# A perceiver layer on one Trainium2 core: order of the work at batch boundaries of the cross attention and at group boundaries of the self attention

## The chip, the cores and the metric

The kernel runs on one core of a Trainium2 chip. The metric is the device time of one execution, in microseconds (us). The kernel before takes 922.68 us (median of 3 runs, 922.39 to 923.87). A core has a matmul engine (PE), a vector engine (DVE), an activation engine (ACT), a general engine (POOL) and a sync engine (SP) that issues DMAs. Each works through its own list of instructions in order; they meet only at semaphores. A semaphore wait holds back everything that stands behind it on its engine.

## The reference

Three stages, each added to x (8 batches of 64 rows by 512):

```python
# cross attention: context of 1601 keys per batch, 16 heads, a latent of 32
C_q = Q @ Wq_d;  C_kv = K @ Wkv_d
scores = einsum('bnhl,bkl->bhnk', (C_q @ W_qk).reshape(b, n, H, LKV), C_kv) / sqrt(LKV)
out = einsum('bhnk,bkhd->bnhd', softmax(scores), (C_kv @ Wv_u).reshape(b, nkv, H, HD))
# self attention: 32 query heads in 8 groups of 4, 512 selected cache keys and 64 new ones
out = softmax(q @ k_full.T / sqrt(HD)) @ v_full;  out @ wo.T
# feed forward, with weights that need a mean over the whole matrix
coeff = mean(abs(w - base));  W = base + coeff * sign(w - base)
out = (silu(h @ W1.T) * (h @ W3.T)) @ W2.T
```

## The kernel before

Everything is written by hand: each engine has one function body per stage, and the order in it is the order on the engine. Most fp32 operands are split in a high and a low part, and products are made of three passes.

**Cross attention.** The loop runs over 8 batches `b`. For a batch there are 13 tiles of keys (`KT`). `scores(b, t)` on PE makes a tile's scores in two halves of 512 columns, `exponential` on ACT turns each half into probabilities, `add_tile` on POOL sums probability tiles in groups (`GROUPED`) for the denominators, and `values(b, units)` on PE multiplies the probabilities with the latent keys. The maximum that is subtracted is not taken from these scores. It is computed one batch ahead: between the tiles of batch `b`, PE makes 16 pairs of products for batch `b + 1` (`max_scores`, called as `maximum(i)`), in two buffers, and DVE reduces each (`take_max`, L1003). When all 16 are reduced, DVE combines them (`negate_max`, L1009), PE turns the result to a row with 8 transposes (`turn_max`, L706), and ACT copies that row of 1024 values, the *shift row*, into the query operand (`shift_row`, L919), where it takes part in `scores` as one more row of the contraction. So `scores(b + 1, 0)` cannot start before the shift row of `b + 1` stands.

At the end of a batch PE also has `compress(b + 3)` (the latent keys of a later batch, only while `b + 3 < 8`), `natural(b + 3)`, and `tail_and_denominators(b)` (L758 and L745), which adds the last tile's values and multiplies all probability sums with ones. The latter waits for POOL's last sum. ACT then copies the denominators (`copy_den`, L926), in the next batch, behind its second tile.

**Self attention.** `head(g, i, ...)` is one step of a pipeline over 32 heads (group `g`, head `i` in it). In a step PE turns the probabilities of the last head (`turn_probs`, L1413 and L1422), makes scores for this one (`score`, L1401), projects queries of the next (`queries`, L1382), and multiplies with the values (`mix`, L1431 to L1440). In the step with `i = 0` of groups 1 to 7, PE also makes the output products of the group before, 48 matmuls (`output`, L1455). I call this the group boundary; there are 7. DVE then adds the four output tiles to x (`add_output`, L1808), and splits the new group's values (`values_low`, L1726 and L1728). POOL casts the values (L1886), waits for `values_low`, and then subtracts three pieces of the feed-forward weights and their bases (`w_piece`, L1908). ACT sums the absolute values of these three pieces (`abs_sum`, L1624) and makes the high part of the first output weight of the group (`output_weight_high`, L1645), which has to wait until the output products no longer read the old one. Behind both stands `turned_high` (L1637) of the next head, on which `turned_low` (DVE, L1742) and PE's third turn depend, since there are two buffers for turned probabilities.

## Time and profile before

| what | value |
|---|---|
| median of 3 runs | 922.68 us |
| profiled execution, its own time | 919.89 us |
| its span | 917.8 us |
| cross attention, batch loop | from about 44 to 286 us |
| keys and norm | 288 to 318 us |
| self attention | 318 to about 796 us |
| feed forward | to the end |
| PE busy | 93% |
| mean granted PE clock, share of 2.4 GHz | 0.985 |

The profile gives, for each instruction group, start, duration, and for an engine that sat idle how long and for whom it waited. A busy PE is not PE at its peak: the ends of matmuls are modelled, and short waits vanish in them. So the distance between starts says more than the busy time.

### The profile page before, as it was taken

The numbers are of one execution on the slowest core, as the hardware profiler recorded it, in microseconds if no ns is written. First come the engines' busy times: TensorE is split into PE (matmuls) and PEld (weight loads), VectorE is DVE, ScalarE is ACT, GpSimd is POOL, SyncE is SP. The second block draws the span as 40 slices with busy tenths as digits, with TensorE's granted clock in tenths as the row PEclk, the third lists the DMA queues.
The fourth block names the chain that finished last, engine by engine and source line by source line (L and its number), as shares of the span: only waits on it lengthen the run. The fifth ranks groups of instructions, "written<-read, shape, count | busy, mean of one in ns | idle before, by whom it ended". The sixth has DMA issues, their size and how long they took to land.

```text
span 917.8 us, 15508 instructions
## 1 busy us (share of the span) xinstructions
PE 851.7 (93%) x5338; PEld 650.9 (71%) x5338; DVE 603.3 (66%) x993; ACT 519.1 (57%) x1005; POOL 459.6 (50%) x294
## 2 busy tenths in 40 slices
PE   6898899888987889999999999999999999899998
PEld 4455455544433668888788887887878878788886
DVE  5965567555625268578486684776848759768884
ACT  5655546555554466386474774655746657555552
POOL 2698788786751054544444444345454454154430
PEclk9899999999999999999999999999999999999999
DMA  8654244104103515032050230501505002535531
GB/s 359 217 199 153 99 153 171 28 19 136 58 1 121 193 43 207 24 134 97 0 206 23 95 133 0 206 23 41 187 0 203 15 0 92 184 127 194 192 107 46
DMA packets 42338, 102.96 MB, mean 112 GB/s; under 512 B 7858, under 2 KB 12978, under 8 KB 41394
## 3 DMA queue, kind: packets, MB, share of 16 engines
q1 hardware_dynamic: 42002, 102.06, 31.7%
q8 instruction: 30, 0.49, 0.2%
q10 hardware_dynamic: 288, 0.26, 0.1%
q14 instruction: 18, 0.15, 0.1%
HBM read 96.95 MB, written 1.05 MB: 107 GB/s over the span
## 4 chain that ended last, share of the span: by engine, by line
PE 51%; POOL 5%; DVE 3%; issue 3%; ACT 2%; DMA 0%; SPq 0%; DVEq 0%; POOLq 0%; ACTq 0%
PE psum L1401 9%; PE psum L1382 9%; PE psum L1517 8%; PE psum L1413 5%; PE psum L1531 4%; POOL w_piece L1908 3%; PE psum L1440 3%; PE psum L1431 3%; PE psum L1455 3%; PE psum L1436 3%; ACT w_piece L1624 2%; PE psum L1422 1%; PE psum L1432 1%; PE psum L1434 1%; DVE probs_t_low L1742 1%
## 5 line engine op out<-in xcount | busy, mean ns | idle before, releaser
L1896 POOL TENSOR_TENSOR head_probs<-head_probs,inverse_den 128x576 f32<-128x576 f32 x128 | 147.5, 1153 | 203.7 <-DVE inverse_den L1749 203.7
L1003 DVE TENSOR_REDUCE max_part<-psum 128x1 f32<-128x804 f32 x128 | 121.2, 991 | 38.4 <-PE psum L698 38.0
L901 ACT ACTIVATE probs<-psum 128x512 f32<-128x512 f32 (+1 forms) x208 | 106.7, 608 | 47.4 <-PE psum L719 46.4
L1631 ACT ACTIVATE head_probs<-psum,neg_max 128x576 f32<-128x576 f32 x128 | 94.7, 740 | 46.2 <-DVE neg_max L1766 45.8
L1766 DVE TENSOR_REDUCE neg_max<-psum 128x1 f32<-128x576 f32 x128 | 96.9, 757 | 23.8 <-PE psum L1401 21.3
L567 POOL TENSOR_TENSOR prob_sums<-prob_sums,probs 128x1024 f32<-128x1024 f32 (+1 forms) x42 | 100.2, 2386 | 18.4 <-ACT probs L901 14.1
L1742 DVE TENSOR_TENSOR probs_t_low<-psum,probs_t_high 128x512 fp32r<-128x512 f32 x124 | 84.8, 684 | 16.6 <-ACT probs_t_high L1637 15.6
L1413 PE MATMUL psum<-ident,head_probs 128*128 128x128 f32 x496 | 78.7, 274 | 16.5 <-DVE probs_t_low L1742 15.1
L719 PE MATMUL psum<-q_t,c_t 97*128 97x512 f32 (+1 forms) x208 | 76.1, 445 | 14.2 <-ACT q_t L919 7.1
L1401 PE MATMUL psum<-k_high,query_t_high 128*128 (+1 forms) x256 | 86.5, 338 | 1.9 <-DVE query_t_low L1721 1.4
L567 POOL TENSOR_TENSOR prob_sums<-probs 128x1024 f32<-128x1024 f32 x30 | 71.3, 2380 | 23.9 <-ACT probs L901 23.8
L1413 PEld LDWEIGHTS psum<-ident,head_probs 128*128 128x128 f32 x496 | 60.6, 141 | 28.5 <-issue 20.2
L1916 POOL TENSOR_TENSOR ffn_quant<-ffn_raw 128x1536 f32<-128x1536 f32 x13 | 45.6, 3510 | 67.4 <-DVE ffn_w_low L1830 26.9
L1401 PE MATMUL psum<-k_high,query_t_low 128*128 (+1 forms) x256 | 75.7, 296 | 0.0
L698 PE MATMUL psum<-c_t,q_t 96*128 96x402 f32 x256 | 73.5, 374 | 2.3 <-DVE max_part L1003 1.7
L1401 PE MATMUL psum<-k_low,query_t_high 128*128 (+1 forms) x256 | 75.6, 295 | 0.0
L1637 ACT ACTIVATE probs_t_high<-psum 128x512 fp32r<-128x512 f32 x124 | 72.9, 588 | 0.5 <-PE psum L1422 0.5
L698 PEld LDWEIGHTS psum<-c_t,q_t 96*128 96x128 f32 x256 | 43.9, 191 | 37.8 <-DVE max_part L1003 23.3
L719 PEld LDWEIGHTS psum<-q_t,c_t 97*128 97x128 f32 (+1 forms) x208 | 38.5, 191 | 38.0 <-ACT probs L901 27.8
L1908 POOL TENSOR_TENSOR w_piece<-w_piece 128x1024 f32<-128x1024 f32 x21 | 49.7, 2397 | 23.6 <-DVE value_low L1728 23.6
L1645 ACT ACTIVATE wo_t_high<-wo_nat 128x512 fp32r<-128x512 f32 x32 | 20.0, 626 | 72.4 <-PE psum L1455 72.4
L1808 DVE TENSOR_TENSOR x<-psum,x 128x512 f32<-128x512 f32 x32 | 22.1, 690 | 46.9 <-PE psum L1455 46.9
(227 smaller groups left out, 1948.2 us busy)
## 6 DMA issues: line engine op xcount, KB each, us to landing
ctx_t_odd<-in_ctx_dram SPq DMA_DIRECT2D x4, 3202.0 KB, 11.0
ffn_raw<-in_L_ffn_w_dram SPq DMA_DIRECT2D x42, 256.0 KB, 3.9
ffn_raw<-in_L_ffn_mean_w_dram SPq DMA_DIRECT2D x42, 256.0 KB, 4.1
w_piece<-in_L_ffn_w_dram SPq DMA_DIRECT2D x21, 512.0 KB, 6.5
w_piece<-in_L_ffn_mean_w_dram SPq DMA_DIRECT2D x21, 512.0 KB, 7.5
cache<-in_ctx_dram SPq DMA_DIRECT2D x3, 3202.0 KB, 10.8
wq_nat<-in_L_attn_wq_dram SPq DMA_DIRECT2D x32, 256.0 KB, 7.4
wo_nat<-in_L_attn_wo_dram SPq DMA_DIRECT2D x32, 256.0 KB, 3.2
```

Source lines behind the costliest of these rows:

```text
L567: pool.tensor_tensor(total[rows, :], (prob_buffer(b, t - 1) if first else total)[rows, :], prob_buffer(b, t)[rows, :], ALU.add).then_inc(s ...
L698: mm = pe.matmul(psum[:, bank + k, 0:PIECE_KEYS], q_t[0:SHIFT, b, 2 * qt:2 * qt + 2, :].rearrange("p h n -> p (h n)"), c_t[0:SHIFT, b % 3, ...
L719: pe.matmul(psum[0:rows_of(t), n % SCORE_BANKS, :], lhs, rhs[:, half * BANK:(half + 1) * BANK], start=True, stop=True).then_inc(s_sb, 1)
L901: act.activation(prob_buffer(b, t)[0:rows, half * BANK:(half + 1) * BANK], psum[0:rows, n % SCORE_BANKS, :], ACT.Exp, scale=XSCALE).then_i ...
L1003: dve.tensor_reduce(max_part[:, qt, pair:pair + 1], psum[:, bank:bank + 2, 0:PIECE_KEYS], AX.XY, ALU.max).then_inc(s_max, 1)
L1382: mm = pe.matmul(psum[:, head_bank(i), :], wq_t[a][:, c, :], (xh, xl)[b][:, c, :], start=(k == 0), stop=(k == 3 * DC - 1))
L1401: mm = pe.matmul(psum[:, bank, 0:HALF], q_t[a][:, qt * P:(qt + 1) * P], (k_high, k_low)[b][:, keys], start=(step == 0), stop=(step == 2))
L1413: mm = pe.transpose(bank[:, t * P:(t + 1) * P], probs[:, qt, t * P:(t + 1) * P], core.ident[:, :])
L1631: act.activation(probs[:, qt, :].rearrange("p (a k) -> p a k", a=2), psum[:, 2 * (qt % 2):2 * (qt % 2) + 2, 0:HALF], ACT.Exp, bias=neg_max ...
L1742: dve.tensor_tensor(probs_t[1][:, 0:ST, qt * P:(qt + 1) * P], psum[:, turn_bank(qt), :].rearrange("p (t q) -> p t q", t=ST), probs_t[0][:, ...
L1766: dve.tensor_reduce(neg_max[:, qt:qt + 1], psum[:, 2 * (qt % 2):2 * (qt % 2) + 2, 0:HALF], AX.XY, ALU.max, negate=True).then_inc(s["max"], 1)
L1896: pool.tensor_tensor(probs[:, qt, :], probs[:, qt, :], rden[:, qt:qt + 1].to_broadcast([P, KEYS]), ALU.mult).then_inc(s["norm"], 1)
```

## The change

Four edits, all of order.

1. Group boundary, ACT: the three absolute sums stand ahead of the output weight's high part. Group boundary, DVE: `values_low` stands ahead of all four `add_output`.
2. Cross attention, shift row: PE signals after the first four transposes and after the last four. ACT copies the row as two halves of 512. `scores(b, 0)` waits, half by half, for the half that it reads.
3. Cross attention, maxima: from `maximum(5)` on, each is issued one place earlier; one pair instead of two stands behind the last `values` of a batch.
4. Batches 5, 6 and 7: `tail_and_denominators(b)` stands ahead of `turn_max(b + 1)`, and ACT copies these denominators at the end of the batch, ahead of the shift row. Batches 0 to 4 keep `tail_and_denominators` behind the first scores of the next batch.

```diff
@@ tensor engine, turn_max
-                mm.then_inc(s_mt, 1)
+                    if qt % 4 == 3:
+                        mm.then_inc(s_mt, 1)
@@ tensor engine, scores
-                    if t == 0 and half == 0:
-                        pe.wait_ge(s_shift, b + 1)
+                    if t == 0:
+                        pe.wait_ge(s_shift, 2 * b + half + 1)
@@ tensor engine, batch loop
                 maximum(4)
+                maximum(5)
                 values(b, range(0, 2))
                 for t in range(6, 10):
-                    maximum(t - 1)
+                    maximum(t)
                     scores(b, t)
-                maximum(9)
+                maximum(10)
                 values(b, range(2, 4))
                 for t in range(10, KT):
-                    maximum(t)
+                    maximum(t + 1)
                     scores(b, t)
-                maximum(KT)
+                maximum(KT + 1)
                 values(b, range(4, 6))
-                maximum(KT + 1)
                 maximum(KT + 2)
                 if b + 3 < BATCH:
                     compress(b + 3)
-                if lead:
                     turn_max(b + 1)
-                if b + 3 < BATCH:
                     natural(b + 3)
+                else:
+                    tail_and_denominators(b)
+                    if lead:
+                        turn_max(b + 1)
                 if lead:
                     scores(b + 1, 0)
                     scores(b + 1, 1)
-                tail_and_denominators(b)
+                if b + 3 < BATCH:
+                    tail_and_denominators(b)
@@ activation engine, shift_row
-                act.wait_ge(s_mt, b + 1)
-                act.activation(q_t[SHIFT:STACK, b, :, :].rearrange("p (a h) n -> p a (h n)", a=2),
-                               psum[SHIFT:STACK, TURN_BANK:TURN_BANK + 2, :], ACT.Copy).then_inc(s_shift, 1)
+                for half in range(2):
+                    heads = slice(half * XH // 2, (half + 1) * XH // 2)
+                    act.wait_ge(s_mt, 2 * b + half + 1)
+                    act.activation(q_t[SHIFT:STACK, b, heads, :].rearrange("p h n -> p (h n)"),
+                                   psum[SHIFT:STACK, TURN_BANK + half, :], ACT.Copy).then_inc(s_shift, 1)
@@ activation engine, batch loop
-                    if t == 1 and b > 0:
+                    if t == 1 and 0 < b < BATCH - 2:
                         copy_den(b - 1)
...
                 if b + 3 < BATCH:
                     compressed(b + 3)
+                else:
+                    copy_den(b)
                 if b + 1 < BATCH:
                     shift_row(b + 1)
...
-            copy_den(BATCH - 1)
@@ activation engine, head
-                if this and i == 0:
-                    output_weight_high(g, i)
                 if last and i == 0:
                     for k in range(3):
                         abs_sum(g, k)
+                if this and i == 0:
+                    output_weight_high(g, i)
@@ vector engine, head
-                if i == 0 and last:
-                    add_output(g, 0, turn_bank(0))
                 if this and i == 0:
                     values_low(g)
                 if i == 0 and last:
-                    for qt in range(1, TT):
+                    for qt in range(TT):
                         add_output(g, qt, turn_bank(qt))
```

The other waits on `s_mt` and `s_shift` have their counts doubled. Line numbers below the edits move by a few.

On ACT, at the last group boundary (`w_piece...` are the absolute sums, `wo_t_high` the output weight, `mixed_t_high` the result of `mix`, `probs_t_high` the turned probabilities), before:

```order
L1583 ACTIVATE wq_t_high<-wq_nat 128x512
L1612 ACTIVATE mixed_t_high<-psum 128x512
L1645 ACTIVATE wo_t_high<-wo_nat 128x512
L1624 ACTIVATE w_piece_4090,abs_part<-w_piece_4090 128x1024
L1624 ACTIVATE w_piece_4091,abs_part<-w_piece_4091 128x1024
L1624 ACTIVATE w_piece,abs_part<-w_piece 128x1024
L1637 ACTIVATE probs_t_high<-psum 128x4x128
```

and now:

```order
L1590 ACTIVATE wq_t_high<-wq_nat 128x512
L1619 ACTIVATE mixed_t_high<-psum 128x512
L1631 ACTIVATE w_piece_4114,abs_part<-w_piece_4114 128x1024
L1631 ACTIVATE w_piece_4115,abs_part<-w_piece_4115 128x1024
L1631 ACTIVATE w_piece,abs_part<-w_piece 128x1024
L1652 ACTIVATE wo_t_high<-wo_nat 128x512
L1644 ACTIVATE probs_t_high<-psum 128x4x128
```

The output weight has moved behind the three sums; nothing else moved.

On DVE, at the same boundary (`x<-psum,x` is `add_output`), before:

```order
L1734 TENSOR_TENSOR mixed_t_low<-psum,mixed_t_high 128x512
L1808 TENSOR_TENSOR x<-psum,x 128x512
L1726 TENSOR_TENSOR value_low<-cache,value_high 128x512
L1728 TENSOR_TENSOR value_low<-v_new,value_high 64x128
L1808 TENSOR_TENSOR x<-psum,x 128x512 x3
L1766 TENSOR_REDUCE neg_max<-psum 128x1
```

and now:

```order
L1741 TENSOR_TENSOR mixed_t_low<-psum,mixed_t_high 128x512
L1733 TENSOR_TENSOR value_low<-cache,value_high 128x512
L1735 TENSOR_TENSOR value_low<-v_new,value_high 64x128
L1813 TENSOR_TENSOR x<-psum,x 128x512 x4
L1773 TENSOR_REDUCE neg_max<-psum 128x1
```

The low values no longer stand behind the first output tile.

On PE, at the end of batch 5 (L733 is the last `values`, `c_t,q_t` with 402 columns are the maxima, `max_row` the turn, `c_nat` and `ones_by_latent` behind it the tail and the denominators), before:

```order
L733 MATMUL psum<-probs,c_nat 32x512 x8
L698 MATMUL psum<-c_t,q_t 128x402 x4
L706 MATMUL psum<-ident,max_row 97x128 x8
L719 MATMUL psum<-q_t,c_t 128x512 x4
L758 MATMUL psum<-probs,c_nat 32x512
L745 MATMUL psum<-prob_sums,ones_by_latent 32x512
L758 MATMUL psum<-probs,c_nat 32x512
L745 MATMUL psum<-prob_sums,ones_by_latent 32x512 x9
L698 MATMUL psum<-c_t,q_t 128x402 x2
```

and now:

```order
L734 MATMUL psum<-probs,c_nat 32x512 x8
L698 MATMUL psum<-c_t,q_t 128x402 x2
L759 MATMUL psum<-probs,c_nat 32x512
L746 MATMUL psum<-prob_sums,ones_by_latent 32x512
L759 MATMUL psum<-probs,c_nat 32x512
L746 MATMUL psum<-prob_sums,ones_by_latent 32x512 x9
L706 MATMUL psum<-ident,max_row 97x128 x8
L720 MATMUL psum<-q_t,c_t 128x512 x4
L698 MATMUL psum<-c_t,q_t 128x402 x2
```

Twelve matmuls went from behind the next batch's first scores to ahead of the turn, and one pair of maxima went ahead of the values.

## Rows read from the trace of the kernel before

**Rows 1.** First part of the page: busy us, share, instructions.

```profile
PE 851.7 (93%) x5338; PEld 650.9 (71%) x5338; DVE 603.3 (66%) x993; ACT 519.1 (57%) x1005; POOL 459.6 (50%) x294
```

**Rows 2.** Chain that ended last, in order of time: start, duration, what.

```profile
420.97 2.05 PE psum L1382 x9
...
432.30 2.06 PE psum L1382 x9
...
456.73 2.05 PE psum L1382 x9
```

**Rows 3.** Timeline, one group boundary: start, duration, engine, what, [idle before <-releaser].

```profile
438.22 0.69 DVE L1734 TENSOR_TENSOR mixed_t_low<-psum,mixed_t_high 128x512 fp32r<-128x512 f32 x1 [1.69 <-ACT mixed_t_high L1612]
...
440.31 0.69 DVE L1808 TENSOR_TENSOR x<-psum,x 128x512 f32<-128x512 f32 x1 [1.40 <-PE psum L1455]
...
441.52 0.28 DVE L1728 TENSOR_TENSOR value_low<-v_new,value_high 64x128 fp32r<-64x128 f32 x1
441.96 7.11 POOL L1908 TENSOR_TENSOR w_piece<-w_piece 128x1024 f32<-128x1024 f32 x3 [3.37 <-DVE value_low L1728]
...
448.28 0.60 PE L1413 MATMUL psum<-ident,head_probs 128*128 128x128 f32 x4
...
448.54 0.63 ACT L1645 ACTIVATE wo_t_high<-wo_nat 128x512 fp32r<-128x512 f32 x1 [10.35 <-PE psum L1455]
...
452.20 0.58 ACT L1637 ACTIVATE probs_t_high<-psum 128x512 fp32r<-128x512 f32 x1
...
453.64 0.63 PE L1413 MATMUL psum<-ident,head_probs 128*128 128x128 f32 x4 [2.06 <-DVE probs_t_low L1742]
```

**Rows 4.** Waits of the whole span: us in total, times, longest.

```profile
PE psum L1413 <- DVE probs_t_low L1742: 15.1, 9, 2.1
```

**Rows 5.** Windows: length, busy us (instructions) PE PEld DVE ACT POOL, granted clock, DMA.

```profile
437.39:448.28 10.89, 10.89 (x50) 8.96 (x48) 3.56 (x6) 0.60 (x1) 7.17 (x5) 1.00 0.00 0
549.10:575.00 25.90, 23.84 (x119) 20.32 (x119) 12.22 (x22) 12.12 (x27) 13.15 (x10) 0.94 0.00 0
```

**Rows 6.** Timeline of a batch boundary that stands for batches 0 to 4.

```profile
130.10 1.00 PE L698 MATMUL psum<-c_t,q_t 96*128 96x402 f32 x4
130.77 1.90 DVE L1003 TENSOR_REDUCE max_part<-psum 128x1 f32<-128x804 f32 x2 [1.42 <-PE psum L698]
131.82 2.79 PE L650 MATMUL psum<-ctx_t_odd,wkv_d 128*32 128x384 f32 x32 [0.72 <-DVE max_part L1003]
...
134.99 1.12 PE L706 MATMUL psum<-ident,max_row 128*97 128x128 f32 x8
...
136.15 1.02 ACT L919 ACTIVATE q_t<-psum 1x1024 fp32r<-1x1024 f32 x1 [0.47 <-PE psum L706]
...
137.31 0.94 PE L719 MATMUL psum<-q_t,c_t 97*128 97x512 f32 x3 [0.70 <-ACT q_t L919]
```

**Rows 7.** Timeline of the boundary from batch 5 to batch 6.

```profile
222.16 2.34 POOL L567 TENSOR_TENSOR prob_sums<-prob_sums,probs 65x1024 f32<-65x1024 f32 x1
...
224.56 1.12 PE L706 MATMUL psum<-ident,max_row 128*97 128x128 f32 x8 [1.83 <-DVE max_row L1009]
...
226.88 2.16 PE L719 MATMUL psum<-q_t,c_t 97*128 97x512 f32 x4 [1.20 <-ACT q_t L919]
...
227.59 2.08 ACT L901 ACTIVATE probs<-psum 128x512 f32<-128x512 f32 x4 [0.86 <-PE psum L719]
...
229.84 2.58 PE L745 MATMUL psum<-prob_sums,ones_by_latent 128*32 128x512 f32 x17
...
232.50 1.21 ACT L926 ACTIVATE u_all<-psum 64x512 f32<-64x512 f32 x2 [2.83 <-PE psum L745]
...
234.38 0.50 PE L719 MATMUL psum<-q_t,c_t 97*128 97x512 f32 x1 [0.71 <-ACT probs L901]
```

**Rows 8.** Window in that boundary, columns as in Rows 5.

```profile
226.98:230.40 3.42, 3.42 (x12) 1.30 (x16) 0.00 (x0) 2.08 (x4) 0.65 (x1) 0.50 0.56 182
```

**Rows 9.** Timeline of the boundary from batch 6 to batch 7.

```profile
264.92 0.50 PE L719 MATMUL psum<-q_t,c_t 97*128 97x512 f32 x1 [1.06 <-ACT probs L901]
```

More of the change, by code:

```diff
@@ L679, in max_scores @@
                     pe.wait_ge(s_qlo[b > 1], 2 * (b // 2 if b > 1 else 1))
-                    wait(pe, s_shift, b)
+                    wait(pe, s_shift, 2 * b)
                 elif i == 1 and b == 0:
@@ L772, in mix @@
                 elif b + 1 < BATCH:
-                    pe.wait_ge(s_shift, BATCH)
+                    pe.wait_ge(s_shift, 2 * BATCH)
                 else:
@@ L1007, in negate_max @@
                 dve.wait_ge(s_max, MAXIMA * (b + 1))
-                wait(dve, s_mt, b)
+                wait(dve, s_mt, 2 * b)
                 dve.tensor_reduce(max_row[:, :, SHIFT], max_part[:, :, :], AX.X, ALU.max,
```

## The prediction

> **What bounds the kernel now.** I read the busy shares first: PE is busy 93% of the span, the next engine 66% [rows 1]. So a change pays where PE waits, or where another engine paces PE. The chain in order of time then shows where PE's rhythm breaks. In the self attention the last nine query matmuls of a head start every 11.33 us (420.97 to 432.30); across a group boundary the distance is 24.43 us (432.30 to 456.73) [rows 2]. The 48 output matmuls explain 10.89 us of it [rows 5]. 24.43 - 11.33 - 10.89 leaves 2.21 us, of which 2.06 us shows as PE's wait ahead of the third turn, at 453.64 [rows 3]. The list of waits has this pair with 15.1 us in 9 waits, longest 2.1 [rows 4]: 7 boundaries at about 2.06 us make 14.4 of them.
>
> The timeline tells why. ACT is idle 10.35 us until the outputs are done, makes the output weight at 448.54, then the three sums, and reaches the turned probabilities at 452.20 only [rows 3]. PE made them at 448.28. ACT does work here that could have been done while it sat idle.
>
> In the cross attention the timeline of a batch boundary shows PE waiting 0.72 us for a DVE maximum before `compress` and 0.70 us for the shift row [rows 6]. At the end of batch 5 there is no `compress` to cover the maxima: PE waits 1.83 and 1.20 us there and 0.71 us for an exponential held up by the denominators' copy [rows 7].
>
> **Group boundary.** `mixed_low` runs at 438.22 and takes some 0.6 us. `values_low` now follows it: start about 438.83. Before, 441.52 + 0.28 is its end and POOL starts 0.16 later; from the first half's start (0.6 before 441.52, so 440.92) to POOL is 1.04 us. So POOL starts at about 439.87 in place of 441.96, and its three differences (7.11 us) end at 446.98 [rows 3]. From 448.54 to 452.20 ACT makes the weight copy and three sums, 3.66 us: 0.54 and three times 1.04. So each sum now waits for its difference and the last ends at 446.98 + 0.1 + 1.04 = 448.1, ahead of 448.54, where ACT starts the weight copy anyway. The copy ends at 449.08 and turned probabilities start there in place of 452.20: 3.12 us earlier [rows 3]. PE's wait was 2.06, so it goes, with 1.0 us to spare. What is late next is PE itself. The first output tile is added to x at 440.31 as before, since `values_low` ends at 439.7, so PE's third output tile is not held up. Behind the sums on ACT now stands the weight copy, and behind it the turned probabilities; a late third difference would be covered by 0.4 us of ACT's wait and then by that 1.0. I take 2.2 us for each of 7 boundaries, 15.4 us. Bounds: 7 x 2.06 = 14.4 when only the shown wait goes, and above 1.4 us more, since between 549.10 and 575.00 one boundary took 25.90 us with a granted clock of 0.94 [rows 5] in place of 24.43: a dip of the clock to 1.2 GHz just behind this wait. Lower bound: 1.0 us for each, 7 us, if something unseen stands behind.
>
> **Maxima moved up.** DVE needs 0.95 us for a maximum (1.90 for two) and sets the pace between the `values`; each `values` leaves it idle 1.42 us whatever stands ahead, as PE is in order [rows 6]. So DVE's last maximum does not end earlier. What changes is the end on PE: the last `values` now begins and ends about 0.95 us later (131.05 in place of 130.10), but one pair stands behind it, 0.4 us, not two and a wait. `compress` starts at 131.45 in place of 131.82: 0.37 us, bounded by 0 and by the wait of 0.72. This counts for batches 0 to 4. The scores of tiles 10 to 12 come 0.9 us later by it; POOL's sums have slack there in those batches.
>
> **Shift row by halves.** Before, the row is copied from 136.15 to 137.17 and the scores start at 137.31, with PE's turn begun at 134.99 [rows 6]. The first four transposes are done about 0.45 earlier than the last, so the first half can start at about 135.7 (ACT's copy of the compressed keys ends there too). A half of 512 costs 0.54 to 0.60: the two copies of 64x512 take 1.21 [rows 7]. Both are done at 136.8 to 136.9, and the first score goes at 136.5, when `natural` lets PE go. From there ACT's exponentials pace the start, which come 1.02 + 136.15 - 136.8 = 0.4 earlier. I take 0.42; bounds 0 and the wait of 0.70. Batches 0 to 4: 5 x (0.37 + 0.42) = 4.0 us, and 0.3 for the very first row; bounds 0 and 7.1.
>
> The Trainium skill (ScalarE: Activation LUTs, What ACT_TABLE_LOAD costs) has an ACTIVATE with immediate scale at 186 ns + 0.833 ns per element. It agrees with the row of 1.02 us for 1024, and it speaks against the split: two halves would be 1.22 us, 0.2 more than one. By it the term would be 0.25 and not 0.42 at each of 7 rows, 1.2 us in all.
>
> **Late denominators, batches 5 and 6.** First the price. PE now waits for POOL's last sum ahead of the turn. That sum ends at 222.16 + 2.34 = 224.50, and comes 0.9 later because its scores do: 225.4 [rows 7]. The last group of denominator matmuls follows. The matmuls take 0.15 us a record with a part of them at half clock (17 in 2.58), 8 records to a group, so 1.2; I take 0.9 at full clock [rows 7]. The turn starts at 226.4 in place of 224.56. ACT copies denominators from 226.55 to 227.78 (1.21) and only then the half rows, so the first score starts at 228.5, not 226.88: 1.6 us worse. Then the return. Behind the first four scores there are no denominators, and ACT goes from exponential to exponential at 0.52 (four in 2.08) without a copy between. The last score of tile 3 waits for the fifth exponential: 229.0 + 5 x 0.52 + 0.2 = 231.8, against 234.38 [rows 7]. Gain 2.6 us. At the next boundary that last score stands 30.54 later, at 264.92, so the same chain gives 262.3; there is no maximum between the scores, which saves 0.5 more: 261.8 [rows 9], gain 3.1. Together 5.7 us. Bounds: the shown waits on ACT's copy and PE alone, 1.2 each, 2.4; and 1.0 more than I take if the clock stays up. Between 226.98 and 230.40 it was at 0.50 [rows 8], the level of 1.2 GHz, after the two waits of 1.83 and 1.20 us.
>
> What follows the batch loop starts its loads behind a barrier, so gains there pass on whole.
>
> **The sum.** 15.4 + 4.0 + 0.3 + 5.7 = 25.4 us. On the profiled execution's own time, 919.89, that is 894.5. The median of the runs is 922.68, 0.3% above it, and I take the gain off that: 897.3. Some runs may hold more clock dips at boundaries, like the one above, which would go too; I say 897.
>
> **Rivals.** (a) *Only the group boundary pays.* Cross attention gives back what it gains: DVE's pace is unchanged and the late denominators hold the turn. For it: the first score of batch 6 is 1.6 us later by my own sum. Against it: 3 us of PE work and a 1.2 us copy leave the stretch behind it. 922.7 - 15.4 = 907.
>
> (b) *The group boundary pays half.* The turned probabilities are early, but PE then waits for DVE, which has a row maximum ahead of the low part. For it: DVE makes a row maximum ahead of the low part, so an early ACT need not mean an early PE. Against it: the 24 ordinary heads have the same order and next to none of these waits [rows 4]. 7 x 1.1 + 10 = 17.7: 905.
>
> (c) *Slower: POOL's differences and DVE's additions get in each other's way.* POOL now runs beside three additions all through, and ACT's weight copy, the turned probabilities and PE stand behind the third sum. If each difference took twice as long, the third ended at 454.1, turned probabilities started at 455.8, 3.6 us later than before; 7 x 3.6 - 10 = 15 us slower, 938. It turns to slower when the third difference ends some 5 us later than I have it. Against it: the 7.11 us were measured beside three such additions already [rows 3].
>
> **How the numbers follow.** Forecast as worked out (892 to 903): 0.75. (a) and (b), 903 to 908: 0.18. Less than that gained, still faster by over 0.2%: 0.03. No change within 0.2% (about what a measurement of this kernel can tell from none; its three runs spread by 0.16%): 0.02. (c) and other slower ends: 0.02. Faster 0.96. The range of 891 to 906 leaves out some 0.2.
>
> **What would show it.** In the profile after, the distance of the query matmuls across a group boundary should be 22.2, with no wait of PE for `probs_t_low`; POOL's differences should start 2.1 us earlier against the outputs. A batch period should be 29.75 in place of 30.55. At the late boundaries PE should wait for a sum of POOL, then for the half rows. I am wrong if the boundary distance stays above 23, or if batches 5 to 7 take as long as before.

## The result and the profile after

The changed kernel takes 899.44 us (median of 4 runs, 895.99 to 901.27), the kernel before 923.27 us beside it (median of 4, 922.39 to 924.5): a ratio of 0.9737, 95% interval 0.9704 to 0.9769. The forecast was 897.0 in 891 to 906. The profiled execution is the slowest of the four, 901.27 us with a span of 899.2, while that of before, at 919.89, was faster than all the timed ones of before. So the two profiles differ by 18.6 us and the medians by 23.8.

The page of the profile after, its first part (busy us, share, instructions) and its chain by engine; before is [rows 1]:

```profile
PE 855.6 (95%) x5338; PEld 652.4 (73%) x5338; DVE 606.5 (67%) x993; ACT 522.6 (58%) x1013; POOL 459.1 (51%) x294
...
PE 60%; DVE 2%; POOL 1%; DMA 1%; ACT 1%; issue 0%; SPq 0%; POOLq 0%; DVEq 0%
```

The same work stands in a shorter span: 8 more ACTIVATEs (the halves), and PE 2 points busier.

**Group boundary.** The chain in order of time (start, duration, what), to be laid beside [rows 2]:

```profile
416.90 2.06 PE psum L1389 x9
...
428.24 2.05 PE psum L1389 x9
...
450.44 2.06 PE psum L1389 x9
```

11.34 us in a head as before, 22.20 across the boundary where it was 24.43. All seven measure 22.19 to 22.20. The timeline of that boundary (start, duration, engine, what, [idle before <-releaser]) answers to [rows 3]:

```profile
434.16 0.69 DVE L1741 TENSOR_TENSOR mixed_t_low<-psum,mixed_t_high 128x512 fp32r<-128x512 f32 x1 [1.68 <-ACT mixed_t_high L1619]
...
435.36 0.28 DVE L1735 TENSOR_TENSOR value_low<-v_new,value_high 64x128 fp32r<-64x128 f32 x1
435.80 7.11 POOL L1913 TENSOR_TENSOR w_piece<-w_piece 128x1024 f32<-128x1024 f32 x3 [1.28 <-DVE value_low L1735]
436.24 0.69 DVE L1813 TENSOR_TENSOR x<-psum,x 128x512 f32<-128x512 f32 x1 [0.61 <-PE psum L1462]
...
442.95 1.06 ACT L1631 ACTIVATE w_piece<-w_piece 128x1024 f32<-128x1024 f32 x1 [1.21 <-POOL w_piece L1913]
...
444.21 0.60 PE L1420 MATMUL psum<-ident,head_probs 128*128 128x128 f32 x4
444.47 0.63 ACT L1652 ACTIVATE wo_t_high<-wo_nat 128x512 fp32r<-128x512 f32 x1 [0.37 <-PE psum L1462]
445.01 0.58 ACT L1644 ACTIVATE probs_t_high<-psum 128x512 fp32r<-128x512 f32 x1
```

POOL starts 1.64 us behind `mixed_low`'s start, where it was 3.74, and takes 7.11 us as before. The last sum is over 0.37 us before the weight copy, whose wait is for PE. The turned probabilities follow PE's first turn by 0.80 us (445.01 less 444.21) in place of 3.92 [rows 3]. In the list of waits (us in total, times, longest) [rows 4] became two short waits, and what was ACT's idle time has a new name:

```profile
ACT w_piece L1631 <- POOL w_piece L1913: 45.6, 21, 4.1
...
PE psum L1420 <- DVE probs_t_low L1749: 0.8, 2, 0.6
```

**Batch boundary, batches 0 to 4.** The same engines as in [rows 6]:

```profile
130.96 1.92 PE L734 MATMUL psum<-probs,c_nat 128*32 128x512 f32 x16
132.82 0.63 PE L698 MATMUL psum<-c_t,q_t 96*128 96x402 f32 x2
133.38 2.79 PE L650 MATMUL psum<-ctx_t_odd,wkv_d 128*32 128x384 f32 x32
...
136.55 1.12 PE L706 MATMUL psum<-ident,max_row 128*97 128x128 f32 x8
...
137.27 1.07 ACT L925 ACTIVATE q_t<-psum 1x512 fp32r<-1x512 f32 x2
...
138.09 1.09 PE L720 MATMUL psum<-q_t,c_t 97*128 97x512 f32 x3
```

Neither wait of PE is left, neither the 0.72 ahead of `compress` nor the 0.70 for the row. The score starts 1.54 us behind the turn, not 2.32.

**Boundary from batch 5 to 6,** answering to [rows 7]:

```profile
222.90 2.36 POOL L567 TENSOR_TENSOR prob_sums<-prob_sums,probs 65x1024 f32<-65x1024 f32 x1
...
225.32 1.07 PE L746 MATMUL psum<-prob_sums,ones_by_latent 128*32 128x512 f32 x8 [0.35 <-POOL prob_sums L567]
226.31 1.12 PE L706 MATMUL psum<-ident,max_row 128*97 128x128 f32 x8
226.45 1.21 ACT L932 ACTIVATE u_all<-psum 64x512 f32<-64x512 f32 x2 [5.20 <-PE psum L746]
227.68 1.07 ACT L925 ACTIVATE q_t<-psum 1x512 fp32r<-1x512 f32 x2
228.41 1.66 PE L720 MATMUL psum<-q_t,c_t 97*128 97x512 f32 x4 [0.98 <-ACT q_t L925]
...
230.28 1.75 PE L720 MATMUL psum<-q_t,c_t 97*128 97x512 f32 x4
```

The turn is at 226.31 (forecast 226.4), ACT's copy at 226.45 (226.55), the first score at 228.41 (228.5). Batch 4's denominators are copied 0.16 us earlier than before (201.81 against 201.97), so the times of the two profiles can be laid side by side here. The last score of tile 3 ends at 232.03, before at 234.88 (234.38 and 0.50) [rows 7]; against the copy that starts the stretch in the table below that is 2.7 us earlier. The window of [rows 8] now holds a full clock. But one batch later the clock falls (windows: length, busy us (instructions) of PE, PEld, DVE, ACT, POOL, granted clock, DMA):

```profile
226.98:230.40 3.42, 2.43 (x12) 1.43 (x10) 0.00 (x0) 3.20 (x8) 0.00 (x0) 1.00 0.52 169
...
258.00:266.00 8.00, 8.00 (x52) 4.26 (x56) 1.05 (x3) 4.86 (x10) 6.79 (x3) 0.57 0.01 2
```

**Where the 18.6 us of the two profiles went.** Each stretch is the difference of two starts in the timeline or the chain: the first copy of compressed keys in the batch loop (52.18 before, 55.34 after), the copy of batch 4's denominators early in batch 5 (201.97, 201.81), the table load of the next stage (288.25, 285.08), the first and the 29th group of nine query matmuls. The later columns are the same stretches in kernels described below.

| stretch, us | before | after | one pair, single run (e7) | one pair, timed (e12) | late as before, timed (e13) | combined (e10) |
|---|---|---|---|---|---|---|
| start to first key copy | 52.18 | 55.34 | 54.97 | 54.14 | 53.53 | 54.88 |
| to batch 4's denominators, some five periods | 149.79 | 146.47 | 146.10 | 146.06 | 146.50 | 146.09 |
| to the next stage's table load | 86.28 | 83.27 | 79.59 | 83.97 | 83.43 | 81.13 |
| to the first query group | 51.72 | 52.99 | 50.61 | 51.71 | 50.39 | 53.00 |
| to the 29th, 7 group boundaries | 410.27 | 393.18 | 393.11 | 393.12 | 392.97 | 393.12 |
| to the end of the span | 167.56 | 167.95 | 168.22 | 168.80 | 167.78 | 167.88 |

After less before: +3.16, -3.32, -3.01, +1.27, -17.09, +0.39: -18.6. The second stretch is the same within 0.5 us in every kernel with the same order of work in it, and so is the fifth where the group boundary has its new order (392.9 to 393.2 us, e5 left out). With the old order the fifth holds one or two dips of the clock: 410.3 us before and in e6, 412.0 in e2. The other stretches differ by up to 4.4 us even between two runs of one program.

### The profile page after: what moved, and what is told of

Its sections match the earlier page's. It is cut to its first block, busy times and chain, and to the rows that moved or that the text cites. A ratio compares the mean times of both kernels' runs of the same rounds, so it can differ in the third digit from the quotient of the medians.

```text
span 899.2 us, 15523 instructions
## 1 busy us (share of the span) xinstructions
PE 855.6 (95%) x5338; PEld 652.4 (73%) x5338; DVE 606.5 (67%) x993; ACT 522.6 (58%) x1013; POOL 459.1 (51%) x294
## 4 chain that ended last, share of the span: by engine, by line
PE 60%; DVE 2%; POOL 1%; DMA 1%; ACT 1%; issue 0%; SPq 0%; POOLq 0%; DVEq 0%
PE psum L1408 11%; PE psum L1389 10%; PE psum L1524 9%; PE psum L1462 8%; PE psum L1420 6%; PE psum L1538 4%; PE psum L1447 3%; PE psum L1438 3%; PE psum L1443 3%; PE psum L1429 1%; PE psum L1441 1%; PE psum L1439 1%; DMA ffn_raw<-in_L_ffn_mean_w_dram 1%; POOL head_probs L1901 0%; POOL ffn_quant L1921 0%; POOL ffn_raw L1921 0%
## 5 line engine op out<-in xcount | busy, mean ns | idle before, releaser
L1010 DVE TENSOR_REDUCE max_part<-psum 128x1 f32<-128x804 f32 x128 | 121.1, 991 | 41.5 <-PE psum L698 41.1
L720 PE MATMUL psum<-q_t,c_t 97*128 97x512 f32 (+1 forms) x208 | 78.0, 449 | 8.4 <-ACT probs L905 5.7
L698 PE MATMUL psum<-c_t,q_t 96*128 96x402 f32 x256 | 75.3, 377 | 4.2 <-DVE max_part L1010 3.6
L1408 PEld LDWEIGHTS psum<-k_high,query_t_high 128*128 128x128 f32 x256 | 48.3, 189 | 2.7 <-DVE query_t_low L1728 1.8
```

Of the source, the lines that this page charges most:

```text
L698: mm = pe.matmul(psum[:, bank + k, 0:PIECE_KEYS], q_t[0:SHIFT, b, 2 * qt:2 * qt + 2, :].rearrange("p h n -> p (h n)"), c_t[0:SHIFT, b % 3, ...
L720: pe.matmul(psum[0:rows_of(t), n % SCORE_BANKS, :], lhs, rhs[:, half * BANK:(half + 1) * BANK], start=True, stop=True).then_inc(s_sb, 1)
L1010: dve.tensor_reduce(max_part[:, qt, pair:pair + 1], psum[:, bank:bank + 2, 0:PIECE_KEYS], AX.XY, ALU.max).then_inc(s_max, 1)
L1408: mm = pe.matmul(psum[:, bank, 0:HALF], q_t[a][:, qt * P:(qt + 1) * P], (k_high, k_low)[b][:, keys], start=(step == 0), stop=(step == 2))
```

## The experiments

Medians are of 4 runs and ratios are to the kernel before, timed beside them, unless the text says otherwise. A single run gives a time and a profile, but no interval.

**e1_group_only.** The kernel before with the two edits at the group boundary and nothing else.
```diff
-                if this and i == 0:
-                    output_weight_high(g, i)
                 if last and i == 0:
                     for k in range(3):
                         abs_sum(g, k)
+                if this and i == 0:
+                    output_weight_high(g, i)
```
(and the same hunk of `values_low` as in the change.)

> The kernel before with the two edits of the group boundary alone. Theory (the boundary pays 2.2 us, seven times): query matmuls 22.2 us apart across a boundary, no wait of PE for the low probabilities, and the whole faster by 15.4 us, ratio 0.983; up to 1.5 us more where the kernel before had a dip of the clock there. Rival (b) of the prediction (it pays half): distance 23.3, ratio 0.992.

Measured: 906.02 us against 924.11 (13 runs), 0.9802 (0.9774 to 0.983). All seven distances are 22.2, so rival (b), 23.3, falls. The stage of the seven boundaries takes 392.99 us. The median gain, 18.1 us, is above the theory's 15.4 and the 1.5 for a dip; the theory's ratio of 0.983 lies at the upper end of the interval.

**e2_cross_only.** The changed kernel with the group boundary as before (the hunk above undone on both engines).

> The changed kernel with the group boundary as in the kernel before, so only the three edits of the cross attention. Theory: batches 0 to 4 gain 0.67 us each (read from the profile after), the late boundaries up to 5.7 less what half clock in the last batch takes back, 2: in all 6 to 9 us, ratio 0.990 to 0.993. Rival (a) (the cross attention gives back what it gains): ratio 0.998 to 1.000. The distance of the query matmuls across a group boundary stays 24.4.

Measured: 917.82 us (10 runs), 0.9931 (0.9896 to 0.9965). Boundaries at 24.4, two at 25.9. The two gains, 18.1 and 6.3 us, make 24.4, the whole change 23.8: within the intervals they add up.

**e5_low_values_late, e6_sums_late.** The two halves of the group boundary's edit, each undone alone in the changed kernel, a single run each. e5 puts `values_low` behind the first output tile's addition again:
```diff
-                if this and i == 0:
-                    values_low(g)
                 if i == 0 and last:
-                    for qt in range(TT):
+                    add_output(g, 0, turn_bank(0))
+                if this and i == 0:
+                    values_low(g)
+                if i == 0 and last:
+                    for qt in range(1, TT):
```

> The changed kernel with the low values again behind the first output tile; the absolute sums stay ahead of the weight. Theory (POOL's third difference then ends at 449.1 on the clock of the kernel before, the sum at 450.2, the weight copy at 450.8, PE's third turn at 452.2): PE waits 0.6 us for the low probabilities, distance across a boundary 22.8. Rival (only the place of the sums counts, the low values are free to stand anywhere): 22.2. Rival (the low values carry it all): 24.4.

> The changed kernel with the output weight ahead of the absolute sums again; the low values stay ahead of the output tiles. Theory (ACT still starts its three sums only when the outputs are done, at 449.08): no gain at the boundary, distance 24.4 and PE's wait 2.06, though POOL's differences start 2.1 us earlier. Rival (POOL's earlier start pays by itself): a distance under 23.5.

Measured: e5 908.22 us, boundaries 22.84 to 22.98, the seven-boundary stage 398.17, 5.0 us longer than in the changed kernel. The distances are near the theory's 22.8, and both rivals fall. Its stretch behind batch 4 is 4.4 us longer too (87.70 against 83.27): the clock fell at both late boundaries, which this edit doesn't touch. e6, with the output weight ahead of the sums again, 917.10 us and 24.4 (one of 25.76). Their waits, e5's and then e6's:

```profile
PE psum L1420 <- DVE probs_t_low L1749: 4.5, 9, 0.6
```
```profile
PE psum L1420 <- DVE probs_t_low L1749: 15.2, 9, 2.1
```

With the weight first, the low values' move gains nothing: the wait is that of [rows 4] within 0.1 us. With the sums first, the wait falls to 0.6, and the low values' move takes that. So the sums' order is worth 1.5 us a boundary and the low values 0.7 on top, in this order only.

**e4_maxima_as_before, e8_row_whole.** In the changed kernel, the PE order of the maxima as before, and the shift row copied in one piece; a single run each.
```diff
-                for half in range(2):
-                    heads = slice(half * XH // 2, (half + 1) * XH // 2)
-                    act.wait_ge(s_mt, 2 * b + half + 1)
-                    act.activation(q_t[SHIFT:STACK, b, heads, :].rearrange("p h n -> p (h n)"),
-                                   psum[SHIFT:STACK, TURN_BANK + half, :], ACT.Copy).then_inc(s_shift, 1)
+                act.wait_ge(s_mt, 2 * b + 2)
+                act.activation(q_t[SHIFT:STACK, b, :, :].rearrange("p (a h) n -> p a (h n)", a=2),
+                               psum[SHIFT:STACK, TURN_BANK:TURN_BANK + 2, :], ACT.Copy).then_inc(s_shift, 2)
```

> The changed kernel with the maxima placed as in the kernel before. Theory: the steady batch period is 30.55 - 0.42 = 30.1 us (29.88 in the changed kernel), PE waits 0.72 us for a maximum ahead of the compress again, and at the late boundary POOL's last sum is 0.8 us earlier, so the first score of batch 6 comes 0.8 us earlier. Rival (the maxima carry the batch's gain, the halves nothing): period 30.5. Rival (the maxima cost more than they bring): period at or under 29.9.

> The changed kernel with the shift row copied whole, by one activation. Theory: the period is 0.3 to 0.4 us longer than the changed kernel's 29.88, and PE waits 0.7 us for the row at each boundary. Rival (the fixed price of a second activation eats the gain): the same period within 0.1.

Measured: 899.04 and 906.97 us. The batch period is 30.55 before, 29.88 after, 30.16 in e4 and 30.35 in e8. So, each with the other in place, the maxima are worth 0.28 and the halves 0.47 a batch; that makes 0.75, and the two together moved the period by 0.67. In e4 the first score of batch 6 comes 0.33 us earlier against the copy of batch 4's denominators (26.27 us behind it, 26.60 in the changed kernel), not the 0.8 that was expected. The old waits are back, in e4 and in e8 (timelines, PE):

```profile
133.03 2.79 PE L650 MATMUL psum<-ctx_t_odd,wkv_d 128*32 128x384 f32 x32 [0.73 <-DVE max_part L1010]
```
```profile
136.55 0.93 PE L720 MATMUL psum<-q_t,c_t 97*128 97x512 f32 x3 [0.76 <-ACT q_t L923]
```

e8's total is 7.5 us above the changed kernel's median and 5.7 above its profiled run, and its periods account for 2.3; the stretch behind batch 4 takes 90.0 us, against 83.3, with dips of the clock at both late boundaries.

**e7_one_pair_only, e12_one_pair_timed.** One program, run twice: only the pair of maxima ahead of the last `values` is moved up, the other five stay where they were.
```diff
                 maximum(4)
-                maximum(5)
                 values(b, range(0, 2))
                 for t in range(6, 10):
-                    maximum(t)
+                    maximum(t - 1)
                     scores(b, t)
-                maximum(10)
+                maximum(9)
                 values(b, range(2, 4))
                 for t in range(10, KT):
-                    maximum(t + 1)
+                    maximum(t)
                     scores(b, t)
+                maximum(KT)
                 maximum(KT + 1)
```

> The changed kernel in which only the last but one pair of maxima is moved ahead of the last values; all others stand as in the kernel before. Theory (what pays is that one pair and not two stands behind the last values): period 29.9 as in the changed kernel, and the late scores no longer come 0.9 us later. Rival (two pairs in a row ahead of the last values make PE wait a step of DVE, 0.95 us, that the gain does not cover): period over 30.2.

> The kernel in which only one pair of maxima is moved up (ahead of the last visits to the values) and the rest is as in the changed kernel; seen once at 894.7 us with a batch period of 29.80, now timed in rounds. Theory A (moving the other five pairs makes each visit to the values wait for VectorE's maximum, 0.08 us a batch, nothing else): 5 periods by 0.08 us, 0.4 us below the changed kernel's 899.4, that is 899; the 894.7 was a run with few dips of the clock. Theory B (the shorter wait of TensorE at the boundaries also keeps its clock up): 895 to 896 as the median, and the changed kernel is beaten by 3 to 4 us.

Measured: 894.71 us in the single run, 899.54 (896.56 to 903.05) timed, 0.9745 (0.9702 to 0.9788): the same as the changed kernel. The period is 29.80 in the single run's profile and in the timed one alike, 0.08 less than with six pairs moved, and the first score of batch 6 comes 0.6 us earlier against the copy of batch 4's denominators than in the changed kernel (0.9 was expected). So one pair does all that moving the maxima does. The 894.7 was luck: the two profiles of this one program differ by 5.2 us, 4.4 of them behind batch 4 (79.59 against 83.97 in the table). The last batch in the single run (e7), then in the timed profile (e12) (windows, columns as before):

```profile
256.00:264.00 8.00, 7.55 (x61) 3.42 (x61) 1.05 (x3) 5.99 (x13) 6.97 (x3) 1.00 0.01 2
264.00:272.00 8.00, 7.69 (x42) 2.63 (x46) 0.00 (x0) 5.88 (x12) 7.16 (x4) 1.00 0.00 0
```
```profile
256.00:264.00 8.00, 8.00 (x54) 3.64 (x54) 1.05 (x3) 3.94 (x8) 7.01 (x3) 0.57 0.01 2
264.00:272.00 8.00, 7.78 (x31) 2.57 (x27) 0.00 (x0) 4.25 (x9) 4.68 (x2) 0.79 0.00 0
```

Up to there the two agree: from turn to turn 27.19 us in both, the first score of batch 7 then 2.11 and 2.10 us behind its turn. Then one run stays at 1.00 and the other falls to 0.5. Whoever had compared single runs would have called this a gain of 5 us.

**e3_late_as_before, e13_late_timed.** Again one program twice: the changed kernel with the late denominators as before.
```diff
                 if b + 3 < BATCH:
                     compress(b + 3)
+                if lead:
                     turn_max(b + 1)
+                if b + 3 < BATCH:
                     natural(b + 3)
-                else:
-                    tail_and_denominators(b)
-                    if lead:
-                        turn_max(b + 1)
                 if lead:
                     scores(b + 1, 0)
                     scores(b + 1, 1)
-                if b + 3 < BATCH:
-                    tail_and_denominators(b)
+                tail_and_denominators(b)
```

> The changed kernel with the late denominators (batches 5 to 7) placed as in the kernel before. Theory: from the sixth batch's start to the end of the cross attention it takes some 5 us more than the changed kernel, 2.7 of it at the boundary from batch 5 to 6 where PE waits 1.8 us for the row of maxima and the exponentials are held up by the denominators' copy. Rival (a): the difference is under 1 us, since the turn no longer waits for POOL's sum. Clock: if the two waits of PE ahead of the first scores (1.8 and some 0.7 us) bring the clock down, it is at 1.2 GHz behind the boundary from 5 to 6 here and not in the changed kernel.

> The changed kernel with the late denominators as before (copied behind the second exponential of the next batch, products behind the first scores), seen once at 899.1 us, now timed in rounds. Theory A (as predicted, the reorder is worth 2.6 us at the boundary from batch 5 to 6 and 3.1 at the next): 899.4 and 5.7 us, 905. Theory B (the waits removed at the two boundaries are given back by the clock and by ScalarE's copy ahead of the half rows): 899 to 900, no difference to the changed kernel.

Measured: 899.10 us in the single run, 897.57 (896.65 to 898.6) timed, 0.9726 (0.9696 to 0.9757). Theory A, 905, falls, and so does the "some 5 us" that was expected of the single run: the stretch behind batch 4 takes 83.7 and 83.4 us in the two, 83.3 in the changed kernel. The boundary from 5 to 6 without the reorder but with halves and moved maxima (timeline of the timed profile, PE):

```profile
222.59 1.12 PE L706 MATMUL psum<-ident,max_row 128*97 128x128 f32 x8 [1.29 <-DVE max_row L1012]
224.04 1.66 PE L720 MATMUL psum<-q_t,c_t 97*128 97x512 f32 x4 [0.33 <-ACT q_t L922]
...
226.10 2.31 PE L746 MATMUL psum<-prob_sums,ones_by_latent 128*32 128x512 f32 x17
...
228.81 0.85 PE L720 MATMUL psum<-q_t,c_t 97*128 97x512 f32 x3
...
230.36 0.50 PE L720 MATMUL psum<-q_t,c_t 97*128 97x512 f32 x1 [0.70 <-ACT probs L902]
```

PE's waits of 1.83 and 1.20 us [rows 7] are 1.29 and 0.33 here, and the clock in the windows from 222 to 252 us is 1.00 in both runs. From the denominators' copy of batch 5 to that of batch 6 it takes 28.47 us, 30.54 in the kernel before (263.04 less 232.50), and 27.83 in the changed kernel (254.28 less 226.45). Before, then the changed kernel (timelines):

```profile
232.83 0.85 PE L719 MATMUL psum<-q_t,c_t 97*128 97x512 f32 x3
...
263.04 1.21 ACT L926 ACTIVATE u_all<-psum 64x512 f32<-64x512 f32 x2 [3.01 <-PE psum L745]
```
```profile
254.28 1.21 ACT L932 ACTIVATE u_all<-psum 64x512 f32<-64x512 f32 x2 [5.19 <-PE psum L746]
```

Of the 2.7 us that the changed kernel gains there, 2.07 come without the late denominators; these add 0.64. The last score of tile 3 says the same: against the copy of batch 4's denominators it ends 2.08 us earlier than before in e13, and 2.69 in the changed kernel. Where the 2.07 lie can be read too. The first score stands 1.45 us behind the turn, not 2.32: 0.87. From it to the three scores behind the denominators it is 4.77 us (228.81 less 224.04), not 5.95 (232.83 less 226.88) [rows 7]: 1.18, over the same matmuls, which before ran in part at the half clock of [rows 8]. So 0.87 is the row's wait, and 1.18 the dip.

**e10_combined.** One pair moved, and the denominators of batches 5 to 7 copied by VectorE behind the copy of u.
```diff
-                else:
-                    copy_den(b)
...
                 copy_u(b)
+                if b + 3 >= BATCH:
+                    copy_den(b)
```

> The changed kernel with two further edits: of the six pairs of maxima only one is moved up (the one ahead of the last visits to the values), and the denominators of batches 5 to 7 are copied by VectorE behind the copy of u, where ScalarE did it ahead of the shift row. Theory A (ScalarE's copy of 1.21 us stands ahead of the half rows at the three late boundaries, and VectorE's copy beside it costs nothing there): 2 boundaries by up to 1.2 us, so about 2 us below the kernel with one pair moved alone, which showed 894.7 in one look: 892 to 893, and the first score of batch 6 follows the turn by 0.98 us less the copy, some 1.2 us earlier against the batch's start than in the changed kernel. Theory B (VectorE's next maxima are late by its two copies, as they were by each piece of VectorE's work at this place): no gain or a loss of up to 1 us, 895 to 896. Theory C (the lost time at the late boundaries is clock alone): the same as the kernel with one pair, with the stretch from batch 5's denominators to the next stage's table load at 80 to 84 us as the dips have it.

Measured: 896.16 us (894.07 to 898.2), 0.97 (0.9668 to 0.9732). The half rows follow the turn at once, with the first score's wait down to 0.33:

```profile
224.81 1.12 PE L706 MATMUL psum<-ident,max_row 128*97 128x128 f32 x8
226.26 1.66 PE L720 MATMUL psum<-q_t,c_t 97*128 97x512 f32 x4 [0.33 <-ACT q_t L925]
```

The score comes 1.45 us behind the turn, not 2.10. From the turn of batch 6 to that of batch 7 it is 26.53 us, 27.19 in both runs with one pair alone, at a full clock in all three: 0.66, of the 1.2 expected; theory A's total, 892 to 893, isn't reached. Its median is 3.3 us below the changed kernel's, but the intervals overlap, so that it beats it is likely and not shown. VectorE's copy by itself, without the moved pair's change, wasn't tried.

**e11_first_row_whole.** The kernel with one pair, the first batch's row in one piece, the other seven in halves.
```diff
+                if b == 0:
+                    act.wait_ge(s_mt, 2)
+                    act.activation(q_t[SHIFT:STACK, b, :, :].rearrange("p (a h) n -> p a (h n)", a=2),
+                                   psum[SHIFT:STACK, TURN_BANK:TURN_BANK + 2, :], ACT.Copy).then_inc(s_shift, 2)
+                    return
```

> The kernel with one pair of maxima moved, and the first batch's shift row copied whole; the other seven stay in halves. Theory A (the halves of the first row set the chunks of TensorE's work at the start otherwise, and its clock sits at half for longer: the first c_parts come at 53.4 to 55.3 us in all seven kernels with half rows and at 52.0 to 52.2 in the three with the whole row): c_parts at 52.1, and 1.5 to 3 us below the kernel with one pair. Theory B (chance of the run): c_parts anywhere between 52 and 55, no difference to the kernel with one pair.

Measured: 895.69 us (894.32 to 899.9), 0.9718 (0.968 to 0.9755). The first keys' copy is at 55.43, the latest of all: theory A falls. The whole row does not bring the early start back. The median is all the same 3.9 us below that of the kernel with one pair (899.54), more than theory A asked for, but not by its mechanism; the intervals of the two ratios overlap, and the profile, at 894.32 us, is one without a dip in the last batch.

## Why the prediction was right, step by step

**Group boundary, 15.4 forecast: right.** Seven distances went from 24.40 to 24.49 (one 25.90) to 22.20: 7 x 2.24 = 15.7, and 1.4 for the boundary of [rows 5] whose dip of the clock did not come. POOL's start, its unchanged 7.11 us, and the 0.4 us by which the sums beat the weight copy came as worked out. e6 and e5 show the inner order: ACT's order had to go first. Rivals (b) and (c) are out with it: no new wait of PE for DVE took the old one's place, and the three differences took the same 7.11 us at their new place.

**Maxima, 0.37 a batch forecast, 0.28 measured (e4); halves, 0.42 forecast, 0.47 measured (e8).** Together 0.79 forecast, 0.67 measured: a period of 29.88, not 29.75. What I had not priced is the other end of the moved maxima, PE waiting for one more of DVE's ahead of a `values` (after, timeline, PE):

```profile
148.98 0.63 PE L698 MATMUL psum<-c_t,q_t 96*128 96x402 f32 x2 [0.26 <-DVE max_part L1010]
```

e7 gets 0.08 us back by not moving those. The halves: 1.07 us for both, against 1.02 for the whole. The Trainium skill (ScalarE: Activation LUTs, What ACT_TABLE_LOAD costs) has, beside the figure that the prediction used, that ACTIVATEs back to back overlap by about 93 ns. The prediction left that out of its 1.22 us. With it the estimate for the two halves is 1.13 us, and the row of 1.07 agrees with that within 0.06.

**The first row, +0.3 forecast: wrong in sign by the profile, and cause open.** The start got 3.16 us longer in the profiled run, and 1.3 to 3.3 in all eleven profiles with halves in the first row or elsewhere; the three with whole rows everywhere have 52.0 to 52.2. In the changed kernel's profile 2.20 us of it lie ahead of the turn already, as the rows below show. Behind the turn's start the first score comes earlier, 1.45 us in place of 3.22 (1.94 in e6 and e13, whose turns took 2.02 us as before's did), but the first key copy comes later, 12.42 us in place of 11.46. The turn, before and then in the changed kernel (timelines, PE):

```profile
40.72 2.02 PE L706 MATMUL psum<-ident,max_row 128*97 128x128 f32 x8 [1.45 <-DVE max_row L1009]
```
```profile
42.92 1.25 PE L706 MATMUL psum<-ident,max_row 128*97 128x128 f32 x8 [1.45 <-DVE max_row L1016]
```

The clock over the changed kernel's start (window, columns as above), and its `compress`:

```profile
44.00:54.00 10.00, 8.49 (x39) 4.18 (x42) 6.89 (x7) 3.96 (x8) 9.78 (x4) 0.50 0.86 331
```
```profile
50.12 4.69 PE L650 MATMUL psum<-cache,wkv_d 128*32 128x384 f32 x32 [1.31 <-DVE max_part L1010]
```

`compress` took 4.69 us, nearly all of it at half clock, where it took 3.34 before. With the turn equally early (40.6 to 40.9 us), the clock was back at full between 49.2 and 49.5 with whole rows (before, e1, e8) and near 52.5 with halves (e6, e13). But in nine other profiles the turn itself came at 41.5 to 43.0, ahead of anything that the edit touches, and e11 among them was late with a whole first row. That the halves lengthen the stretch at half clock is what the five profiles with equal turns suggest; it is not shown.

**Late denominators, 5.7 forecast: the step that failed.** Every time in it for the boundary from 5 to 6 came as said, the turn, the copy and the score, and the last score of tile 3 moved by 2.7 us where I had 2.6. What failed is the assignment. I priced the new order, at full clock, against a boundary of before that held the dip of [rows 8] and a wait for the row that the halves shorten. Without the reorder 2.07 us of the gain are there all the same; the reorder is worth 0.64 us at that boundary, where the clock is full (e3, e13). Taken twice that is 1.3 us, not 5.7, and below my lower bound of 2.4; the second 0.64 is an estimate, since at the next boundary the clock falls in all three profiles (after, e3, e13). In time it is nothing that can be told: 897.57 without it, 899.44 with it. And ACT's copy ahead of the half rows, which I did name as 1.6 us worse, is part of why (e10).

**The sum.** Forecast 25.4, measured 23.8 between medians. The profile gives 17.09 (boundaries and a dip), 3.32 (periods) and 3.01 (late boundaries, 2.7 twice less a dip of some 2.4 in the last batch), less 3.16 (start) and 1.66 (rest): 18.6. The 2.4 is the last batch against that of e7, which has no dip: from the copy of batch 6's denominators to the table load it takes 30.80 us, 28.39 in e7. Rival (a), that the cross attention gives all back, is out by e2's 6.3 us. The group boundary and the periods are where the total was earned as worked out. For the rest, that it came out near is in part luck: the late boundaries gave about what I had, but from the other edits and a dip that went; a dip in the last batch and the longer start took back more than that sum knew of; and the medians lie 5.2 us further apart than the two profiles, which no term of mine explains.

## What to carry to other kernels

Where an engine idles ahead of a burst and then does prepared work inside it, move the work into the idle time, on the engine that holds it first: only then does the earlier input pay. Price each edit against the kernel that has the other edits already, and take the slow clock out of the before stretch first, or the last edit is credited with what the others bring. Count distances that repeat (22.20 seven times), and mistrust the total of a single run: one program gave 894.7 and 903.1 us.

## What the runs showed of the hardware

- **TensorE's clock at the late boundaries.** Between 222 and 252 us it fell to the lower level, 1.2 GHz, in all three kernels with the whole row, behind waits for the row of 1.20 us (before, e1) and 1.41 us (e8). With halves it fell there in one profile of eleven (e5), behind a wait of 0.98 us; it did not in seven others with 0.98 to 0.99 us, nor in the three with 0.33. In the last batch it fell in twelve of the fourteen profiles (not in e7 and e11), at a place that changed from run to run; the same program was at 1.00 or at 0.57 over the same 8 us. Such a dip cost 1.2 us at the boundary from 5 to 6 before and 3.1 in e5 (30.97 us from copy to copy, 27.83 in the changed kernel), 2.4 and 4.4 us in the last batch (after and e12, against e7), and 1.4 us at a group boundary.
- **Small copies of ScalarE.** Two half rows of 1x512 take 1.07 us back to back and one of 1x1024 takes 1.02: splitting costs 0.05 us. In the first batch of most profiles the two stood apart (e12: 43.37 and 44.22) and took 0.59 us each.
